# Load order of adj and x, place of the row statistics, and an earlier group of constants in a four-layer graph network on one core

## The reference

```
L0:  deg = sum(adj.T, axis=1);  d = deg ** -0.5
     x += (d[:,None] * adj.T * d[None,:]) @ (h @ W0) + b0
L1:  head = (adj > 0) / max(norm of its row, 1e-12);  inc = adj + head
     x += (inc @ h) / sum(inc, axis=-1)
L2:  ht = h @ W2, four heads of 256
     e = leaky_relu(src[:,None] + dst[None,:], 0.01) + adj
     x += mean over heads of softmax(e) @ ht
L3:  x += relu(adj @ (step(h) @ sign(W3).T))
```

## Time and profile before

| | us |
|---|---|
| median of three runs | 771.5 (770.08 to 772.02) |
| the profiled execution | 770.67 |
| its span, first to last instruction | 768.8 |

### The profile page before, as it was taken

How to read it: one execution, slowest core, us unless ns; L and a number is a source line. 1 busy time by engine, 2 the same in 40 slices (tenths; PEclk the granted TensorE clock), 3 DMA queues, 4 the chain that set the end, 5 groups by cost and what they waited for, 6 DMA issues and landing times.

```text
span 768.8 us, 16799 instructions
## 1 busy us (share of the span) xinstructions
PE 729.3 (95%) x6808; PEld 619.3 (81%) x6808; DVE 667.2 (87%) x1207; ACT 458.7 (60%) x861; POOL 57.1 (7%) x87
## 2 busy tenths in 40 slices
PE   3998999989999999699999999999999999999898
PEld 3665788978888888345888888888888888888787
DVE  6887885889999997378999999999999999997583
ACT  4995100254555555476655786868686786766651
POOL 3005111101111111000000000000000000000000
PEclk9998999999999999899999999999999999999999
DMA  9986770056766642673111612026111612125592
GB/s 333 323 291 195 80 234 1 2 154 208 228 221 222 220 177 110 222 193 86 51 29 28 191 58 56 18 66 193 28 29 28 192 57 56 29 69 179 192 397 69
DMA packets 44172, 105.98 MB, mean 138 GB/s; under 512 B 3072, under 2 KB 17984, under 8 KB 39616
## 3 DMA queue, kind: packets, MB, share of 16 engines
q1 hardware_dynamic: 39824, 94.94, 36.8%
q0 software_dynamic: 4272, 9.96, 7.9%
HBM read 78.12 MB, written 18.91 MB: 126 GB/s over the span
## 4 chain that ended last, share of the span: by engine, by line
PE 72%; DVE 3%; issue 1%; ACT 1%; POOL 0%; ACTq 0%
PE ps L730 14%; PE ps L732 14%; PE ps L731 14%; PE ps L680 5%; PE ps L772 4%; PE ps L773 3%; PE ps L627 3%; PE ps L629 3%; PE ps L628 3%; PE ps L603 3%; PE ps L607 3%; PE ps L641 1%; DVE arena L1228 1%; DVE arena L1371 1%; DVE arena L1234 0%
## 5 line engine op out<-in xcount | busy, mean ns | idle before, releaser
L730 PE MATMUL ps<-arena 128*128 128x257 f16 x1024 | 279.9, 273 | 2.2 <-DVE arena L1364 2.2
L732 PE MATMUL ps<-arena 128*128 128x257 f16 x1024 | 279.4, 273 | 0.0
L731 PE MATMUL ps<-arena 128*128 128x257 f16 x1024 | 279.2, 273 | 0.0
L1037 ACT ACTIVATE arena<-arena 128x512 f16<-128x512 f32 x252 | 158.5, 629 | 95.6 <-PE ps L732 53.2
L1357 DVE SCALAR_TENSOR_TENSOR arena<-arena,w_j 128x512 f32<-128x512 f32 x256 | 189.8, 742 | 0.0
L1364 DVE TENSOR_TENSOR arena<-arena 128x512 f16<-128x512 f32 x256 | 175.4, 685 | 3.1 <-ACT arena L1037 2.6
L730 PEld LDWEIGHTS ps<-arena 128*128 128x128 f16 x1024 | 99.9, 98 | 15.4 <-issue 2.7
L731 PEld LDWEIGHTS ps<-arena 128*128 128x128 f16 x1024 | 100.3, 98 | 12.5
L732 PEld LDWEIGHTS ps<-arena 128*128 128x128 f16 x1024 | 99.8, 97 | 13.0
L869 ACT ACTIVATE arena<-ps 128x512 f16<-128x512 f32 x64 | 38.0, 593 | 56.0 <-PE ps L607 55.9
L627 PE MATMUL ps<-arena 128*128 128x257 f16 x256 | 70.3, 274 | 0.0
(11 more groups left out here) (145 smaller groups left out, 1151.2 us busy)
## 6 DMA issues: line engine op xcount, KB each, us to landing
arena<-in_adj_dram SPq DMA_DIRECT2D x32, 512.0 KB, 6.1
arena<-in_adj_dram SPq DMA_DIRECT2D x16, 1024.0 KB, 6.5
adj_t<-arena SPq DMA_DIRECT2D x16, 1024.0 KB, 7.7
arena<-adj_t SPq DMA_DIRECT2D x64, 256.0 KB, 4.1
arena<-adj_t SPq DMA_DIRECT2D x16, 1024.0 KB, 6.5
x<-arena POOLq DMA_DIRECT2D x15, 512.0 KB, 4.5
arena<-u_rows SPq DMA_DIRECT2D x4, 1024.0 KB, 13.7
x<-in_x_dram SPq DMA_DIRECT2D x4, 512.0 KB, 5.6
```

The source lines that it names most:

```text
L730: mm(ps[:, bank, 0:DE], hi, ht_hi[:, head, j, 0:DE], start=s, stop=False)
L731: mm(ps[:, bank, 0:DE], hi, ht_lo[:, head, j, 0:DE], start=False, stop=False)
L732: ins = mm(ps[:, bank, 0:DE], lo, ht_hi[:, head, j, 0:DE], start=False, stop=e)
L1037: nc.scalar.activation(p_hi[:, j % 4, :], prob[:, j % 4, :], copy).then_inc(p_hi_done, 1)
```

## The change

Five edits: SP's queue issues adj halves 0 to 3 in turn with the quarters of x, w0 behind quarter 1, and halves 4 and 5 last. DVE runs x_stats(n) behind adj_low(n) for n = 0 to 3, and x_shift(n - 1) behind adj_low(n) for n = 1 to 4. The row slots are one step later, w0_hi is made behind adj_high(3). POOL sets ones16 and zero16 first, under a semaphore of their own (flat_consts), for which PE's first matmuls wait; PE waits for the other constants (consts, now two) ahead of transposes(0).

```diff
--- before.py
+++ after.py
@@ -199,7 +199,7 @@
 
 
         def row_slot(t):
-            return 2 + (4 * t) // 3
+            return 3 + (4 * t) // 3
 
         ps = ctx.enter_context(nc.psum_tensor("ps", [P, 8, 512], F32))
 
@@ -212,6 +212,7 @@
         w3_in = sem("w3_in")
         w2_in = sem("w2_in")
         consts = sem("consts")
+        flat_consts = sem("flat_consts")
         ident_zero = sem("ident_zero")
         slot_in = [sem(f"slot_in{k}") for k in range(SLOTS)]
         rows_in = [sem(f"rows_in{k}") for k in range(4)]
@@ -326,9 +327,11 @@
                 sp.dma_start(x[:, XP * p:XP * p + XP, :], x_rows[:, XP * p:XP * p + XP, :]).then_inc(x_in[p], 16)
 
             for p in range(4):
+                load_half(p)
                 load_x(p)
-            sp.dma_start(w0_f, w0_d.rearrange("(c p) d -> p c d", p=P)).then_inc(w0_in, 16)
-            for n in range(SLOTS):
+                if p == 1:
+                    sp.dma_start(w0_f, w0_d.rearrange("(c p) d -> p c d", p=P)).then_inc(w0_in, 16)
+            for n in range(4, SLOTS):
                 load_half(n)
             for n in range(SLOTS, HALVES):
                 sp.wait_ge(nat_lo_done, n - SLOTS + 1)
@@ -424,16 +427,16 @@
 
         @block.gpsimd
         def _(pool):
+            nc.gpsimd.memset(ones16[:, :], 1.0).then_inc(flat_consts, 1)
+            nc.gpsimd.memset(zero16[:, :], 0.0).then_inc(flat_consts, 1)
             nc.gpsimd.memset(ident[:, :], 0.0).then_inc(ident_zero, 1)
-            nc.gpsimd.memset(ones16[:, :], 1.0).then_inc(consts, 1)
             nc.gpsimd.memset(neg_half[:, :], -0.5).then_inc(consts, 1)
             pool.wait_ge(ident_zero, 1)
             nc.gpsimd.affine_select(out=ident[:, :], in_=ident[:, :], compare_op=ALU.not_equal, fill=1.0,
                                     base=0, pattern=[[-1, P]], channel_multiplier=1).then_inc(ident_zero, 1)
             pool.wait_ge(ident_zero, 2)
             nc.gpsimd.tensor_copy(ident16[:, :], ident[:, :]).then_inc(consts, 1)
-            nc.gpsimd.memset(zero16[:, :], 0.0).then_inc(consts, 1)
-            pool.wait_ge(consts, 4)
+            pool.wait_ge(consts, 2)
 
 
             for p in range(4):
@@ -498,7 +501,7 @@
         @block.tensor
         def _(pe):
             mm = nc.tensor.matmul
-            pe.wait_ge(consts, 4)
+            pe.wait_ge(flat_consts, 2)
 
 
             def turn_w3():
@@ -519,6 +522,8 @@
                 return ins
 
             def h0_transposes(t):
+                if t == 0:
+                    pe.wait_ge(consts, 2)
                 pe.wait_ge(relu0, t + 1)
                 if t >= 3:
                     pe.wait_ge(h0_lo_done, t - 2)
@@ -826,7 +831,7 @@
 
             for n in range(HALVES):
                 adj_high(n)
-                if n == 2:
+                if n == 3:
                     act.wait_ge(w0_in, 16)
                     nc.scalar.activation(w0_hi, w0_f, copy, scale=W_SCALE).then_inc(w0_hi_done, 1)
                 for t in range(NB):
@@ -1131,13 +1136,12 @@
                                 h0_t[:, t % 3, 0:DC, :].rearrange("p a n -> p (a n)"), ALU.subtract
                                 ).then_inc(h0_lo_done, 1)
 
-            for p in range(4):
-                x_stats(p)
             for n in range(HALVES):
                 adj_low(n)
-                if n in (0, 1):
-                    x_shift(2 * n)
-                    x_shift(2 * n + 1)
+                if n < 4:
+                    x_stats(n)
+                if 1 <= n < 5:
+                    x_shift(n - 1)
                 if n == 4:
                     dve.wait_ge(w0_hi_done, 1)
                     v.scalar_tensor_tensor(w0_lo, w0_f, W_SCALE, w0_hi, ALU.mult, ALU.subtract
```

## The result

The changed kernel takes 775.41 us (median of 20 runs), the kernel before 770.29 in the same comparison: 1.0061 times as long, 95% interval 1.0045 to 1.0076, or +4.7 us. It is slower by more than the 0.3% that can be told. The profiled execution took 777.05, its span 775.2.

The account below looks back on a forecast made before the run. PE, busy 95%, was taken to bound the kernel, with ACT setting the load's pace after the start. Order +0.2 and clock +1.0 gave +1.2 us on 770.67: 771.9, for the median 772.6, range 769.2 to 775.0.

Parts of the forecast that it names:

- likeliest case (+1.2): Whole kernel: load of adj ends later by 0.2 plus 1.0 us, median 772.6; chance 0.42.
- Within 0.3%: Whole kernel: time differs from before by less than a measurement can tell, 2.3 us; chance 0.60.
- Rival B: PE's clock stays at 1.2 GHz until about 28.5 us, perhaps also longer at the tail: 774.2 to 775.7; chance 0.22.
- The term is +0.2 us: Load of adj, new order of loads, DVE and rows: end 0.2 us later, bounds -1.5 and +1.6.
- If it rises about 25 us ... I take 1.0: PE's low clock in the first rows doubles products and transposes, delaying ACT 1.0 us; bounds 0 and 2.5.
- This lead is lost again to PE: ACT's lead of 1.0 plus 0.5 us goes in waits for transposes behind degrees(n-1), which waits for adj_low(n-1).
- The constants: POOL's two earlier memsets cost it nothing; PE's warming matmuls move from 12.1 to about 1.2 us, clock then low, +1.0 us.

Follow-up runs that it names:

- e5: Changed kernel plus unread ones16 matmuls (45, 50, 68, 30, 25, 20) ahead of degrees(0) to (5), to keep PE dense; 1.0034 of before.
- e6: Changed kernel with each pair of transposes one step earlier in PE's list, ahead of degrees(row_slot - 1); 1.0020 of before.
- e1: Changed kernel with only the edit of the constants undone: zero16 last in POOL's list, PE's warming matmuls behind it; 1.0032 of before.
- e2: Kernel before with only the edit of the constants, PE's warming matmuls at 1 to 5 us; 1.0004 of before.
- e10: Kernel before with the hw_copy of odd t given from ACT to DVE; 1.0025 of before.
- e11: Kernel before with the hw_copy of odd t given from ACT to DVE and transposes one step earlier in PE's list; 0.9961 of before.
- e3: Changed kernel with 210 warming matmuls on PE for 50; 1.0077 of before.
- e8: Changed kernel with both the unread filler matmuls ahead of degrees(0) to (5) and the transposes one step earlier; 1.0042 of before.

## Why the prediction was wrong in size

The direction of its likeliest case (+1.2) was right; the size was 4.7. 775.4 lies 0.4 us above the end of the range, which was built on a before of 771.5 where this comparison has 770.3. Within 0.3% had the chance 0.60 and did not come. Rival B, a longer low clock, named 774.2 to 775.7, and the time fell in there, but in part by luck: B made it of 0.2 for the order, 2.5 for the clock and 1.5 at the tail, while the profiles show 3.0 for the order, 2.0 for the clock and nothing at the tail. Step by step:

- **Held.** PE's first matmul at 1.03 (said 1.2), adj_high(0) at 5.44 (4.9), DVE idle 1.16 us ahead of L1121 (1.1), unread pairs of 1.01 before 25, ACT's waits for the transposes behind degrees behind adj_low (said 2.4 us by pure order and more by the clock; 4.1 came up to the tenth adj_high, and 1.85 in e5 without the low clock), and nothing behind 70 us changed its make-up. The last adj_high came at 68.2, not 63 to 65.
- **"The term is +0.2 us".** This is the step that failed most: e5, without the low clock, still loses 3.0 us in the load, outside the bound of +1.6. The term assumed three rates that the new order did not have. Loads at 362 GB/s were 327 up to half 2: 1.2 us late there, 1.4 at half 3 and 1.7 at half 4. POOL came 0.97 late. And rstd at "1.2 each" was an average of 1.06, 1.54, 1.00 and 1.25; two of the changed kernel's took 1.98. Together adj_low(5) started at 23.25 and not 21.5; in e5 at 23.46, and there transposes(3) ended at 28.10 and not 25.95. That these 2 us are the larger part of the 3.0 is worked out from the rows, no run isolates it.
- **"If it rises about 25 us ... I take 1.0".** This term was too small by half. The clock rose at 31.0. Transposes(3) ended at 30.26, where the prediction had 25.95 at the high level and 28.4 as the bound, but only part of this is the clock: in e5 they end at 28.10, so the order made them 2.2 us late and the low clock another 2.2. e5 puts the clock's worth at 2.0 us in the load and 0.27% in time, within the bound of 2.5. I had placed it low because PE would have no gap from 23 us; it had none from 24.5, and 25 to 30 us were still at 1.2 GHz.
- **"This lead is lost again to PE"** was right, and e6 shows it: 3.6 of 5.0 us come back with one line. I used it only to cancel the lead and did not ask what else it would carry. It passes on every delay of DVE to ACT, whose 0.8 us of idleness in before were read as slack in this coupling.
- **The constants.** That PE's early start is what costs, and not a gain, was right: about half of the loss (e1). That it costs next to nothing in time in the old order (e2) was not foreseen and is not explained.

## What to carry to other kernels

Before moving work off an engine or starting it earlier, follow who stands behind whom in the in-order queues: here ACT depended on DVE through a PE queue in which the transposes stood behind a reduction that nobody was waiting for. Take such a coupling out before judging other edits: the same split of the copies was slower with it (e10, +0.25%) and faster without it (e11, -0.39%), both against before. Work that only warmed TensorE at the start was of no use here once PE waited again: 210 matmuls for 50 did not shorten the time (e3).

## What the runs showed of the hardware

- POOL's first instruction behind its memsets started at 10.9 to 13.7 us, whether affine_select or the power, and whatever PE did; with one and the same list of POOL it varied from 11.56 (e3) to 13.22 (e8).
- The same power instruction on 128x4 took 1.0 to 1.06 us, or up to 2.0 when an adj_low was already running on DVE as it began. It then ended 0.86 to 0.87 us behind the end of this adj_low, however late it had begun beside it: begun 0.10 after the adj_low's start it took 1.98 (17.42 to 19.40, the adj_low from 17.32 to 18.54); in before, begun 0.55 after, 1.54 (13.15 to 14.69, the adj_low from 12.60 to 13.82). Begun 0.13 us before adj_low(2) and beside it, it took 1.01 (14.06 to 15.07). The Trainium skill, "GPSIMD Engine Reference", "1. Specifications", says that GpSimd shares its SBUF interfaces with VectorE and contends with its instructions of two SBUF inputs, which adj_low is; the trace agrees for a power that begins in the midst of one, but not for the one that began first.
- The granted clock was 0.50 from 25 to 30 us with PE busy in every microsecond. It fell in a wait of PE or right behind one: at 20.6 (e3) in one of 1.90 us, at 24.5 (e1) behind one of 1.57, at 62.5 (before) in one of 1.70. It did not fall in the waits of 0.84 (e3) and 0.91 (before, ahead of 18.27).
- Transfers with pieces of 1 KB (x) and 4 KB (adj) in turn moved 317 to 331 GB/s in seven kernels; all of x first, 368 to 374 GB/s up to the same byte, in six. The reason was not looked into.
